# A Perceiver block on one core: first cross tile's queries split early, gate/up weights turned by two DMA transposes

## What is computed

```python
x = x + xattn(layernorm(x), ctx_768)     # q = x Wq, k = ctx Wk, v = ctx Wv, softmax(q k / 8) v, Wo, + bo
x = x + attn(layernorm(x))               # self attention over the 32 rows, with a bias by relative position
x = x + ffn(layernorm(x))                # fake-quantized to 8 bits, see below

def ffn(x):
    xq = act_fake_quant(x)                                   # scale = sigmoid(clip) * max|x| / 127
    gate = einsum('bsh,ih->bsi', xq, weight_fake_quant(w_gate))
    up   = einsum('bsh,ih->bsi', xq, weight_fake_quant(w_up))
    h = act_fake_quant(silu(gate) * up)
    return einsum('bsi,hi->bsh', h, weight_fake_quant(w_down))
```

## Time and profile before

| | us |
|---|---|
| three runs | 1572.11, 1572.41, 1574.92 |
| median | 1572.41 |
| the profiled execution, its own time | 1571.98 |
| its span, first to last instruction | 1570.2 |
| PE busy in it | 1533.9 |
| DVE, ACT, POOL busy | 1063.5, 736.5, 371.4 |

### The profile page before, as it was taken

One profiled execution on the slowest core, in us unless ns is written; L12 is line 12 of the kernel. 1 busy time (PEld: TensorE's weight loads), 2 busy tenths in 40 slices (PEclk: granted clock), 3 DMA queues, 4 the chain that ended last, 5 costly groups with the idle time before them and its releaser, 6 DMA issues.

```text
span 1570.2 us, 36060 instructions
## 1 busy us (share of the span) xinstructions
PE 1533.9 (98%) x13794; PEld 1286.7 (82%) x13802; DVE 1063.5 (68%) x2274; ACT 736.5 (47%) x1596; POOL 371.4 (24%) x225
## 2 busy tenths in 40 slices
PE   7999989999999999999999999999999999998989
PEld 6888788899999899988989999888888888886544
DVE  8766677677667766677667767657555664556788
ACT  5444655555545554555455554433223222224755
POOL 1000234343444344443534344400000000000000
PEclk9999999999999999999999999999999999999999
DMA  6799863341433233332344143250220311323022
GB/s 239 317 369 355 316 254 126 140 146 52 140 136 141 68 116 139 139 109 75 139 139 144 53 140 124 82 195 29 94 83 29 122 42 42 115 77 128 1 107 107
DMA packets 78958, 210.74 MB, mean 134 GB/s; under 512 B 5712, under 2 KB 31760, under 8 KB 76048
## 3 DMA queue, kind: packets, MB, share of 16 engines
q1 hardware_dynamic: 78864, 209.39, 37.1%
HBM read 140.42 MB, written 68.94 MB: 133 GB/s over the span
## 4 chain that ended last, share of the span: by engine, by line
PE 89%; issue 6%; DVE 3%; ACT 1%; DMA 0%; SPq 0%; POOLq 0%; POOL 0%
PE psum_o L697 17%; PE psum_s L674 8%; PE psum_q L674 8%; PE psum_q L1538 6%; PE psum_o L1494 6%; PE psum_q L1494 6%; PE psum_q L727 6%; PE psum_t L1570 6%; PE psum_o L562 5%; PE psum_o L712 5%; PE psum_t L685 3%; PE psum_t L643 3%; PE psum_t L594 1%; PE psum_q L594 1%; PE psum_s L1525 1%
## 5 line engine op out<-in xcount | busy, mean ns | idle before, releaser
L697 PE MATMUL psum_o<-pT,c_nat 128*128 128x512 f32 x1152 | 307.4, 403 | 3.4 <-issue 2.4
L697 PEld LDWEIGHTS psum_o<-pT,c_nat 128*128 128x128 f32 x1152 | 204.6, 189 | 40.1 <-DVE pT L962 3.6
L1310 POOL TENSOR_TENSOR c_nat<-c_raw,constants 128x768 fp32r<-128x768 f32 x64 | 93.9, 1467 | 555.3 <-PE psum_o L697 440.7
L1163 DVE TENSOR_SCALAR oT<-psum_o,c_last 128x512 f32<-128x512 f32 x192 | 143.8, 749 | 66.5 <-PE psum_o L697 66.5
L889 ACT ACTIVATE probs<-psum_s,nmax 128x257 f32<-128x257 f32 x128 | 61.1, 477 | 233.0 <-DVE nmax L1178 233.0
L674 PE MATMUL psum_s<-cT,qk 128*128 128x256 f32 (+1 forms) x1152 | 163.8, 287 | 0.5 <-DVE cT L962 0.3
L674 PEld LDWEIGHTS psum_s<-cT,qk 128*128 128x128 f32 x1152 | 150.1, 189 | 6.6 <-issue 0.5
L674 PE MATMUL psum_q<-cT,qk 128*128 128x256 f32 (+1 forms) x1152 | 151.7, 283 | 1.0 <-DVE qk L1097 1.0
L674 PEld LDWEIGHTS psum_q<-cT,qk 128*128 128x128 f32 x1152 | 142.2, 189 | 4.0 <-issue 2.6
L962 DVE TENSOR_TENSOR pT<-psum_t,pT 128x512 fp32r<-128x512 f32 x128 | 87.8, 687 | 71.0 <-ACT pT L780 71.0
L1295 POOL TENSOR_TENSOR c_raw<-c_raw,last_row 128x768 f32<-128x768 f32 x64 | 120.3, 1880 | 29.6 <-DMA last_row<-in_ctx_dram 19.2
(11 more groups left out here) (295 smaller groups left out, 3114.5 us busy)
## 6 DMA issues: line engine op xcount, KB each, us to landing
qk_by_tile<-staged SPq DMA_DIRECT2D x32, 1536.0 KB, 10.2
raw<-qk_by_tile SPq DMA_DIRECT2D x16, 3072.0 KB, 12.6
c_raw<-in_ctx_dram SPq DMA_DIRECT2D x64, 384.0 KB, 3.2
last_row<-in_ctx_dram SPq DMA_DIRECT2D x64, 192.0 KB, 4.4
out_dram<-x_out SPq DMA_DIRECT2D x32, 256.0 KB, 2.0
x_res<-in_x_dram SPq DMA_DIRECT2D x16, 256.0 KB, 2.6
x_in<-out_dram SPq DMA_DIRECT2D x4, 1024.0 KB, 7.7
x_all<-out_dram SPq DMA_DIRECT2D x1, 4096.0 KB, 13.4
```

What stands on the lines that cost most here:

```text
L697: i = pe.matmul(ps[:], c_nat[(b - 1) % 2][:, part, k, m * P:(m + 1) * P], pT[:, moving, k, :], start=(k, part, moving) == (0, 0, 0), stop= ...
L1163: nc.vector.tensor_scalar(oT[:, m, :, (b - 1) % 4, :], ps[:].rearrange("p (s q) -> p s q", q=SQ), c_last[:, (b - 1) % 2, m:m + 1], None, A ...
```

## The change

The line numbers in this section are those of the changed kernel where a row of it is shown. It has two parts and some small moves.

**The first cross tile.** The memory of `qk` and `wq` is laid out anew, `qk` by row group first and `wq` by query block first, so that row group 0 of `qk` covers exactly query blocks 0 to 2 of `wq` and row group 1 blocks 3 to 5. ACT makes the high parts of row groups 0 and 1 inside the last projection group, after query blocks (3, 2) and (3, 5); those of row groups 2 and 3 take the two places in which 0 and 1 stood. POOL makes all four low parts of tile 0 and the one of row group 1 of tile 1; for tile 1 DVE waits for it (`s_qlo`) before row group 2. In b = 0 of tile 0 ACT scales all four row groups, and the two `norm` of DVE go. In b = 1 of tile 0 PE makes the scores of row group 1 before it transposes the probabilities, not after (`late_turn`), with ACT and DVE in the same order.

**The gate/up weights.** The 11 times 8 transposes of PE, the 11 copies of DVE and the bank unit `GUT` go. SP stores the rounded chunk `w_nat` as it is (`gate_up_rounded`, 2 x 1408 x 512 bf16), and in place of the one load there are two DMA transposes, one for gate and one for up, into a `wguT` laid out as partition, weight, k, row. PE waits for both. The order on SP around them stays.

**Small moves in the projection.** In groups 1 and 2 the statistics of the next group are made two tiles after each of query blocks 0 and 1, not all four after block 2 (group 0 keeps its place). In groups 0 to 2 ACT copies both halves of the first product of block 4.

```diff
-        qk = sb("qk", [P, 2, 4, KC, 4, P], F32R)
+        qk = sb("qk", [P, 4, 2, KC, 4, P], F32R)
...
-        wq = early("wq", [P, 2, KD, INNER], F32R)
+        wq = early("wq", [P, KI, 2, KD, P], F32R)
+        assert 2 * KC * 4 * P == 3 * 2 * KD * P
...
-        w_turned = spare("w_turned", [P, 2 * KD, P], BF16)
...
-        wgu_dram = nc.dram_tensor("gate_up_turned", [FC, P, 2 * KD * P], BF16, kind="Internal").ap()
+        wgu_dram = nc.dram_tensor("gate_up_rounded", [2, HID, D], BF16, kind="Internal").ap()
...
-        wguT = sb("wguT", [P, FC, 2, KD, P], BF16)
+        wguT = sb("wguT", [P, 2, KD, HID], BF16)
...
-            pe.wait_ge(s_scaled, 8 * t + 2 * b)
-            pe.wait_ge(s_normed, 8 * t + 2 * b)
+            pe.wait_ge(s_scaled, 8 * t + (2 * b + 2))
+            if section != "first" or b > 1:
+                pe.wait_ge(s_normed, 8 * t + (2 * b - 2))
...
+        def late_turn(b, section):
+            return section == "first" and b == 1
...
-                if before:
+                if before and not late_turn(b, section):
                     pe_probsT(pe, t, b, section)
                 pe_scores(pe, t, b, 1, section)
+                if late_turn(b, section):
+                    pe_probsT(pe, t, b, section)
...
+        def act_takes_both(s, j, c):
+            return s < GROUPS - 1 and (j, c) == (4, 0)
+
         def act_group_qk(act, s, j):
             wait_slot(act, s, j)
             for c in range(KC):
-                ps, free = full(act, project(("QK", s, j, c, 0)))
-                nc.scalar.activation(staged[:, j % 4, :, 0, c * P:(c + 1) * P], tokens_of(ps), ACT.Copy).then_inc(free, 1)
+                for par in range(2 if act_takes_both(s, j, c) else 1):
+                    ps, free = full(act, project(("QK", s, j, c, par)))
+                    nc.scalar.activation(staged[:, j % 4, :, par, c * P:(c + 1) * P], tokens_of(ps), ACT.Copy).then_inc(free, 1)
...
+                    if (s, j) == (GROUPS - 1, 2):
+                        act_qk_high(act, 0, 0)
...
+                    if (s, j) == (GROUPS - 1, 5):
+                        act_qk_high(act, 0, 1)
...
-                        act_qk_high(act, 0, j - 4)
-            for rg in range(2, 4):
-                act_qk_high(act, 0, rg)
+                        act_qk_high(act, 0, j - 2)
...
+                scale(0, 2)
                 exp(0, 3)
+                scale(0, 3)
...
+                if late_turn(b, section):
+                    exp(b, 1)
...
+            if section == "first" and rg == 2:
+                dve.wait_ge(s_qlo, 4 * t + rg)
...
-                    if s < GROUPS - 1 and j == 2:
+                    if s == 0 and j == 2:
                         dve_group_stats(dve, s + 1, x_in)
+                    if 0 < s < GROUPS - 1 and j < 2:
+                        dve_group_stats(dve, s + 1, x_in, slice(2 * j, 2 * j + 2))
...
+                if act_takes_both(s, j, c):
+                    continue
...
-                dve.wait_ge(s_qlo, 2)
-                dve_qk_low(dve, 0, 2)
                 row_max(0, 1)
-                dve_qk_low(dve, 0, 3)
...
-                norm(0, 2)
                 row_max(0, 3)
                 inverse(0, 3)
-                norm(0, 3)
...
-                dve_probsT(dve, t, b, 0, section)
-                row_max(b, 1)
+                if late_turn(b, section):
+                    row_max(b, 1)
...
-                    dve_qk_low(dve, t + 1, 1, section)
...
-            for rg in range(2):
+            for rg in range(4):
                 pool_qk_low(pool, 0, rg)
-            pool.wait_ge(s_qlo, 4)
...
+            full(pool, U1(("S", 3, 1), 0, "first"))
+            pool.wait_ge(s_qlo, 4 + 1)
+            pool_qk_low(pool, 1, 1)
...
-        def pe_turn_weights(pe, c):
-
-            pe.wait_ge(s_wround, c + 1)
-            ps, done = empty(pe, own(("GUT", c)))
-            for w in range(2):
-                for k in range(KD):
-                    m = pe.transpose(bf16_blocks(ps, 2 * D)[:, KD * w + k, :], w_nat[:, w, k * P:(k + 1) * P], ident16[:])
-            m.then_inc(done, 1)
...
-                    full(act, own(("GUT", c - 1)))
+                    act.wait_ge(s_wgu, 16 * c)
...
-        def dve_turned(dve, c):
-
-            if c:
-                dve.wait_ge(s_wgu, 16 * c)
-            ps, free = full(dve, own(("GUT", c)))
-            nc.vector.tensor_scalar(w_turned[:], bf16_blocks(ps, 2 * D), 1.0, None, ALU.mult).then_inc(free, 1)
...
-        def store_turned(sp, c):
-
-            taken(sp, own(("GUT", c)))
-            sp.dma_start(wgu_dram[c], w_turned[:].rearrange("p k n -> p (k n)")).then_inc(s_wgu, 16)
+        def store_rounded(sp, c):
+
+            sp.wait_ge(s_wround, c + 1)
+            sp.dma_start(wgu_dram[:, c * P:(c + 1) * P, :].rearrange("w p d -> p w d"), w_nat[:]).then_inc(s_wgu, 16)
...
-                        sp.dma_start(wguT[:].rearrange("p c w k n -> p c (w k n)"), wgu_dram.rearrange("c p n -> p c n")).then_inc(s_wguback, 16)
+                        for w in range(2):
+                            sp.dma_start_transpose(out=wguT[:, w, :, :], in_=wgu_dram[w]).then_inc(s_wguback, 16)
...
-                    m = pe.matmul(ps[:, part], wguT[:, i, w, k, :], later[:, k, bass.ds(n * 512, part.stop - part.start)],
+                    m = pe.matmul(ps[:, part], wguT[:, w, k, i * P:(i + 1) * P], later[:, k, bass.ds(n * 512, part.stop - part.start)],
...
-            pe.wait_ge(s_wguback, 16)
+            pe.wait_ge(s_wguback, 32)
```

59 lines of the change are left out of this document (27 added, 32 removed).

## The result

The changed kernel takes 1561.3 us (median of four runs, 1560.31 to 1562.87), the kernel before 1572.26 in the same session (1571.32 to 1574.92): a ratio of 0.9928, 95% interval 0.9917 to 0.994. The medians differ by 11.0 us; the ratio, which is worked out from all executions, stands for 11.3 us, its interval for 9.4 to 13.0. The forecast was 1562.9, in a range of 1558 to 1578. Run again later beside other runs of the kernel before, it gave 0.9928 once more (0.9914 to 0.9942). Ratios compare across sessions, medians only within one. One execution of the kernel before in the last session took 3070.84 us and is left out of its figures.

The account below looks back on a forecast made before the run. PE was taken as the bound, busy 1533.9 of 1570.2 us; 6.0 (gate/up) + 0.5 (projection) + 2.6 (first tile after its end) = 9.1 us off 1571.98 gave 1562.9 us, range 1558 to 1578.

Parts of the forecast that it names:

- Gate/up transposes: Self attention's gate/up chunks: taking the transposes off PE saves 0.54 us for each of 11 chunks, 6.0 us (4.6 to 7).
- Projection: Projection: PE's two waits for DVE's copy behind late statistics go, with a copy moved to ACT; 0.5 us (0.2 to 0.9).
- First tile: First cross tile: earlier splits and scales start the first product with the context at 199.2, not 203.00; 3.7 us ahead.
- End of the tile: End of the first cross tile: POOL's low part holds up DVE's two `norm`, so 2.6 us remain of the 3.7.
- DMA transposes: Before the feed forward: the two transposes take up to 25 us, within 28 us of room, so hidden at cost 0.
- (d): Before the feed forward: DMA transposes a little late, between 28 and 41 us together; 1563 to 1575.5 us; chance 0.06.
- (e): Before the feed forward: DMA transposes take longer than 37 us together; at 50 us, 1585 us; chance 0.12.
- (f): Before the feed forward: DMA transposes go block after block, 1.5 us each, 104 us late; 1667 us; chance 0.06.
- The clock: End of the first tile: 1.6 us lost to low clock after PE's 2.44 us wait, expected to stay; plus or minus 1.6.
- (a): Whole kernel: the forecast itself holds, 1561 to 1565 us, likeliest 1562.9; chance 0.45.
- (b): End of the first tile: POOL and DVE don't collide, or low clock doesn't return, or both; 1559.7 to 1561.3; chance 0.18.
- (c): First tile brings only 0 to 1 us, through ACT's load or a late context load; 1564.5 to 1567; chance 0.13.

Follow-up runs that it names:

- the part alone: The kernel before with only the gate/up part (no transposes on PE, rounded chunk stored, two DMA transposes): 1566.97 us, ratio 0.9959.
- The second execution: The changed kernel, unaltered, run and profiled once more: 1562.13 us beside 1573.66, ratio 0.9928.
- the first tile's part alone: The kernel before with the first tile and the small projection moves, gate/up transposes still on PE: 1566.76 us, ratio 0.9962.

## Why the prediction held, and where it did not

**Gate/up transposes: 6.0 forecast, 6.1 and 6.2 measured** (412.07 and, in the part alone, 411.99, against 418.20). The 0.54 us of a chunk, read from three block starts, held for eleven. No wait of ACT for the store appeared. Nothing else of the stage moved.

**Projection: 0.5 (0.2 to 0.9), measured 0.6 to 1.1.** The waits of the earlier trace rows are gone as forecast. They are 0.4 us, so a part of the gain is not in them, and where it lies is open.

**First tile: 3.7 forecast, 4.2 measured.** The mechanism held, and the size was too small: I let the transposes of the probabilities wait for ACT's fourth scale until 196.1. It ended at 195.4, and PE, busy with two score units, started them at 195.61 without a wait. The late turn has 0.85 us of the 4.2; without it that scale does hold PE (0.77 us). By the prediction's own figures the term is 3.8 and not 3.7 (203.00 - 199.2).

**End of the tile: 1.1 lost forecast (3.7 to 2.6), 0.9 measured (4.2 to 3.35).** POOL ended at 225.55 (forecast 225.8), the pair of `norm` at 225.97 (226.4), the row maximum came at 230.88 (231.6) and the wait of 2.44 us was the same. One row of the trace, a `norm` of 1.62 us, was enough to forecast the meeting. The alternative figure, 230.0 if the `norm` were not held up, promised 0.4 us too much: with the `norm` gone DVE waits for POOL's end, and 1.2 us come back, not 1.6. The Trainium skill's rule ("SBUF — State Buffer", section "Who interferes with whom") agrees with 3.12 us beside POOL and 0.61 without it.

**DMA transposes: hidden, as forecast.** Up to 25 us was my reading, 13.9 came. The plain load was the nearer neighbour by far; block after block would have been 132 us. The estimate from the Trainium skill's "DMA: Bandwidth & Descriptors", section "Latency and other measured facts", 11 us, was near. The estimate of 115 us from the Trainium skill's "VectorE: DVE Perf Modes", section "The three transpose paths", took its 1309 ns for each of 88 blocks one after another, and the trace contradicts that: 88 blocks in 13.9 us are 0.16 us each. The rivals (d), (e) and (f) fell together.

**The clock: the term that the sum left out.** The prediction left the low clock at the end of the first tile in, rightly for this execution, and put nothing down for low clock that differs from one execution to the next. The sum of the terms is 9.1 us. The stages gave 9.4 in the first execution (4.2 - 0.9 + 6.1), in which the later start hid the gain of the projection (PE's first transpose starts between 10.84 and 11.90 us in the fourteen traces). With the projection's 0.6 to 1.1 us they hold 10.0 to 10.5. The second execution, whose last stretches ran at the old clock, has a span 9.9 us shorter than that of the kernel before. All of this lies in the interval of the measured 11.3 us, 9.4 to 13.0. The mean granted clock of an execution is known for all but the first session of the kernel before. Where it is 0.996, the kernel before took 1571.9 us in the mean (15 executions of three sessions) and the changed kernel 1561.9 (five of two): at an equal clock 10.0 us remain, and about 1 us of the difference goes with the clock.

What varies is the low clock behind PE's idle places. Before the feed forward it costs 0.4 or 1.9 us. Behind the wait of 2.44 us the 15 tiles take 774.65 us without it, 775.79 to 776.08 with it in eight traces, and 777.22 in one: 0, 1.1 to 1.4, or 2.6 us. Behind the wait of 2.48 us in the first tile it costs 0 or 1.5. This last one the change removed together with its wait, so it may be a part of the 1 us, but that is argued and not shown. The scatter does not tell: the kernel before spreads over 2.3 to 5.6 us in a session, the changed kernel over 2.6 and 1.7 and the first tile's part alone over 1.2, but four variants without that wait spread over 3.3 to 4.0. It would take several traces of the kernel before.

**Rivals and range.** (a) held by its mechanism, and the median of 1561.3 lies near its lower end (1561). The terms were all a little too small (by 0.1, by 0.1 to 0.6 and by 0.8 us), so the forecast owes nothing to errors that cancel. The profiled time of 1560.5 fell into the bounds of (b), though neither of its reasons occurred: POOL and DVE met, and the clock fell behind the wait of 2.44 us. (c) fell: the context loads were in time. The lower end of the range, 1558, was not needed: no execution of the changed kernel came below 1560.3.
